# Attention scores as three bf16 matmuls of split operands instead of one f32 matmul

## The reference

```python
xn = layernorm(x)
def attn(x, norm_w, wq, k_of, v_of, wo, base, mask):      # H=16 heads of 64, 4 kv heads
    h = rmsnorm(x, norm_w)
    q, k, v = heads(h @ wq), heads(k_of(h)), heads(v_of(h))
    q, k = qk_norm(rope(q, base)), qk_norm(rope(k, base))
    scores = einsum('bhqd,bhkd->bhqk', q, repeat(k, 4)) / 8.0
    p = softmax(where(mask, scores, -1e30))
    return x + merge(einsum('bhqk,bhkd->bhqd', p, repeat(v, 4))) @ wo
s = attn(xn, ..., base=1e6, mask=causal)                  # global, k and v from a 256-wide latent
s = attn(s, ..., base=1e4, mask=causal & (i - j < 256))   # local, window of 256
ffn = _bitlinear(silu(_bitlinear(xn, w_gate)) * _bitlinear(xn, w_up), w_down)   # _aq(x) @ _wq(w).T
out = x + s * silu(ffn)
```

## Time and profile before

| | us |
|---|---|
| timed runs (2) | 7324.01 and 7516.66, median 7420.34 |
| profiled execution | 7373.87 |
| its slowest core, first to last instruction | 7372.3 |
| spans of the 8 cores | 7305.0 to 7372.3 |
| TensorE matmul busy | 4583.4 (62% of the span) |
| VectorE busy | 1800.2 (24%) |
| ScalarE busy | 1388.6 (19%) |
| mean granted TensorE clock of the cores | 0.730 to 0.738 |

### The profile page before, as it was taken

How to read it: one execution, slowest core, us unless ns; L and a number is a source line. 1 busy time by engine, 2 the same in 40 slices (tenths; PEclk the granted TensorE clock), 3 DMA queues, 4 the chain that set the end, 5 groups by cost and what they waited for, 6 DMA issues and landing times.

```text
span 7372.3 us, 43512 instructions; the slowest of 8 cores (7305.0 to 7372.3 us)
## 1 busy us (share of the span) xinstructions
PE 4583.4 (62%) x12414; PEld 1823.4 (25%) x12414; DVE 1800.2 (24%) x3044; ACT 1388.6 (19%) x2130; POOL 491.4 (7%) x420
## 2 busy tenths in 40 slices
PE   3567777878988898667777768680004263261734
PEld 0122222322332232222334333240001121120311
DVE  2222212111111111112313132223323441433422
ACT  1111202202312332011213021123321020100201
POOL 0000000000000000000000000000002312113120
PEclk6776777778888888777786868775556686685866
DMA  2100010010010000000010100007753133150423
GB/s 81 40 17 29 15 37 2 13 37 0 3 32 16 1 3 33 22 21 31 15 37 3 49 3 32 18 23 268 253 180 101 42 95 88 40 123 21 120 51 80
DMA packets 284199, 382.68 MB, mean 52 GB/s; under 512 B 144706, under 2 KB 225092, under 8 KB 276292
## 3 DMA queue, kind: packets, MB, share of 16 engines
q1 hardware_dynamic: 243652, 228.89, 10.7%
q0 software_dynamic: 40320, 151.02, 6.4%
HBM read 321.14 MB, written 50.33 MB: 50 GB/s over the span
## 4 chain that ended last, share of the span: by engine, by line
PE 57%; DMA 13%; DVE 12%; ACT 6%; issue 4%; POOLq 3%; DVEq 3%; POOL 1%; SPq 0%; ACTq 0%
PE pb L985 10%; PE pb L1020 7%; PE pb L854 7%; PE pb L892 7%; PE pb L1603 4%; POOLq L172 3%; PE pb L1031 3%; DMA fw<-wdq_scr 3%; PE pb L1070 3%; DVEq L172 2%; PE pb L648 2%; PE pb L587 2%; DMA fw<-wuq_scr 2%; PE pb L651 2%; PE pb L1469 2%
## 5 line engine op out<-in xcount | busy, mean ns | idle before, releaser
L985 PE MATMUL pb<-QT,KG 64*128 64x512 f32 (+3 forms) x1984 | 821.6, 556 | 69.3 <-DVEq L177 57.0
L854 PE MATMUL pb<-xst,wst 128*128 128x512 f32 x1024 | 508.0, 665 | 48.7 <-DVEq L177 41.2
L892 PE MATMUL pb<-AO,wst 128*128 128x512 f32 x1024 | 486.4, 641 | 54.1 <-DMA AO<-xst 54.1
L985 PEld LDWEIGHTS pb<-QT,KG 64*128 64x128 f32 x1984 | 373.9, 214 | 514.0 <-issue 476.3
L1603 PE MATMUL pb<-z,fw 128*128 128x512 f16 x1024 | 298.7, 463 | 264.5 <-DMA fw<-wdq_scr 219.9
L994 ACT ACTIVATE Pt<-pb,consts 128x512 f32<-128x512 f32 (+3 forms) x496 | 287.4, 587 | 664.6 <-PE pb L985 660.1
L1469 PE MATMUL pb<-z,fw 128*128 128x512 f16 x1024 | 313.5, 388 | 145.8 <-DVEq L177 88.4
L994 ACT ACTIVATE lat<-pb,consts 128x384 f32<-128x384 f32 (+3 forms) x496 | 266.9, 556 | 501.7 <-PE pb L985 495.1
L1006 DVE TENSOR_TENSOR Pt<-Pt,tb_mask_diag 128x128 f32<-128x128 f32 x256 | 74.8, 292 | 1021.4 <-ACT Pt L994 1018.7
L1475 PE MATMUL pb<-z,fw 128*128 128x512 f16 x1024 | 312.2, 387 | 0.0
L1070 PE MATMUL pb<-rows,tb_onesq 1*64 1x512 f32 x192 | 172.9, 1061 | 217.9 <-ACT rows L1059 193.2
(11 more groups left out here) (181 smaller groups left out, 4798.5 us busy)
## 6 DMA issues: line engine op xcount, KB each, us to landing
wf<-w_gate SPq DMA_DIRECT2D x16, 2048.0 KB, 9.4
wf<-w_up SPq DMA_DIRECT2D x16, 2048.0 KB, 10.0
wf<-w_down SPq DMA_DIRECT2D x64, 512.0 KB, 4.0
fw<-wdq_scr SPq DMA_DIRECT2D x32, 1024.0 KB, 6.6
wst<-g_wq POOLq DMA_DIRECT2D x32, 512.0 KB, 3.6
wst<-g_wo SPq DMA_DIRECT2D x32, 512.0 KB, 3.3
wst<-l_wq POOLq DMA_DIRECT2D x32, 512.0 KB, 3.6
wst<-l_wo SPq DMA_DIRECT2D x32, 512.0 KB, 3.2
```

The lines of the kernel that those rows point to most:

```text
L854: e.matmul(pb[oc], buf[:, oc * 128:(oc + 1) * 128], xst[:, kc * TW:(kc + 1) * TW], start=f, stop=g),
L892: e.matmul(pb[oc], buf[:, oc * 128:(oc + 1) * 128], AO[:, kc * TW:(kc + 1) * TW], start=f, stop=g),
L985: b=scb: e.matmul(b[0:128, qoff:qoff + N], lhsK, rhsQ, start=True, stop=True), inc="T")
```

## The change

The tiles KG and QT (f32) are replaced by KGh, KGl, QTh and QTl (bf16), of the same size in bytes together. A chunk of K or q is now copied from PSUM into AO (f32), normalized and rotated there, and then split: hi is its copy in bf16, lo is the chunk minus hi, in bf16. The function returns a further value, `split_v`, the commit behind the split; the first scores of kv 0 and of kv 1 wait for it. The score matmul becomes three bf16 matmuls that accumulate in the same bank: Kh·Qh, Kl·Qh, Kh·Ql. In the text the loads of the first two blocks of wo stand ahead of the eight q copies instead of behind them. Changes to debugging paths are left out here.

```diff
@@ -333,9 +334,11 @@
-    st["KG"] = kb.sbuf("KG", [128, 2 * st["s"]], F32, scoped=True)
+    st["KGh"] = kb.sbuf("KGh", [128, 2 * st["s"]], BF16, scoped=True)
+    st["KGl"] = kb.sbuf("KGl", [128, 2 * st["s"]], BF16, scoped=True)
...
-    st["QT"] = kb.sbuf("QT", [128, NC * TW], F32, scoped=True)
+    st["QTh"] = kb.sbuf("QTh", [128, NC * TW], BF16, scoped=True)
+    st["QTl"] = kb.sbuf("QTl", [128, NC * TW], BF16, scoped=True)
@@ -680,6 +685,15 @@  (end of rope_qknorm_sb)
     vfin = kb.commit("vector", "V")
+    if split_out is not None:
+        hi, lo = split_out
+        kb.op("vector", lambda e, ch=chunk, hi=hi: e.tensor_copy(hi, ch))
+        kb.drain("vector")
+        kb.op("vector", lambda e, ch=chunk, hi=hi, lo=lo: e.tensor_tensor(
+            lo, ch, hi, ALU.subtract))
+        spv = kb.commit("vector", "V")
+        return {"t_ind2": tt, "v_final": vfin, "split_v": spv,
+                "chunk_v": (deps["chunk_v"] if deps is not None else vfin)}
@@ -779,9 +794,11 @@  (the same at line 820, local)
             for oc in range(2):
-                kdeps = rope_qknorm(st, pb[4 + oc], t0,
-                                    KG[:, oc * s + t0: oc * s + t0 + TW],
-                                    deps=kdeps)
+                kdeps = rope_qknorm(
+                    st, pb[4 + oc], t0, AO[:, oc * TW:(oc + 1) * TW],
+                    deps=kdeps,
+                    split_out=(KGh[:, oc * s + t0: oc * s + t0 + TW],
+                               KGl[:, oc * s + t0: oc * s + t0 + TW]))
@@ -856,25 +875,29 @@
         kb.wait("vector", "T", kb.val("T"))
-        for oc in range(NC):
-            kb.op("vector", lambda e, oc=oc: e.tensor_copy(
-                QT[:, oc * TW:(oc + 1) * TW], pb[oc]))
-        qv = kb.commit("vector", "V")
         kb.guard("sync", "T")
         wo_toks = {0: kb.dma("sync", wst[:, 0:1024], wo[0:128, :], None),
                    1: kb.dma("sync", wst[:, 1024:2048], wo[128:256, :], None)}
+        for oc in range(NC):
+            kb.op("vector", lambda e, oc=oc: e.tensor_copy(
+                AO[:, oc * TW:(oc + 1) * TW], pb[oc]))
+        qv = kb.commit("vector", "V")
...
-            deps = rope_qknorm_sb(st, t0, QT[:, oc * TW:(oc + 1) * TW],
-                                  deps=deps)
-        emit_sdpa_kv(st, glob, t, 0, deep=False, qready=deps["v_final"])
+            deps = rope_qknorm_sb(
+                st, t0, AO[:, oc * TW:(oc + 1) * TW], deps=deps,
+                split_out=(QTh[:, oc * TW:(oc + 1) * TW],
+                           QTl[:, oc * TW:(oc + 1) * TW]))
+        emit_sdpa_kv(st, glob, t, 0, deep=False, qready=deps["split_v"])
...
-        emit_sdpa_kv(st, glob, t, 1, qready=deps["v_final"])
+        emit_sdpa_kv(st, glob, t, 1, qready=deps["split_v"])
@@ -981,9 +1007,15 @@
-            kb.op("tensor", lambda e, lhsK=lhsK, rhsQ=rhsQ, qoff=qoff, N=N,
-                  b=scb: e.matmul(b[0:128, qoff:qoff + N], lhsK, rhsQ,
-                                  start=True, stop=True), inc="T")
+            kb.op("tensor", lambda e, lhsKh=lhsKh, rQh=rQh, qoff=qoff, N=N,
+                  b=scb: e.matmul(b[0:128, qoff:qoff + N], lhsKh, rQh,
+                                  start=True, stop=False))
+            kb.op("tensor", lambda e, lhsKl=lhsKl, rQh=rQh, qoff=qoff, N=N,
+                  b=scb: e.matmul(b[0:128, qoff:qoff + N], lhsKl, rQh,
+                                  start=False, stop=False))
+            kb.op("tensor", lambda e, lhsKh=lhsKh, rQl=rQl, qoff=qoff, N=N,
+                  b=scb: e.matmul(b[0:128, qoff:qoff + N], lhsKh, rQl,
+                                  start=False, stop=True), inc="T")
```

More of the change, by code:

```diff
@@ L8 @@
 F16 = mybir.dt.float16
+BF16 = mybir.dt.bfloat16
 AF = mybir.ActivationFunctionType
@@ L380, in emit_all @@
             pairs = [(st["outT"][ch * 128:(ch + 1) * 128, 0:TW],
-                      st["QT"][:, ch * TW:(ch + 1) * TW]) for ch in range(NC)]
+                      st["QTh"][:, ch * TW:(ch + 1) * TW]) for ch in range(NC)]
         else:
@@ L398, in emit_all @@
         else:
-            pairs = [(st["outT"][0:128, :], st["KG"][:, 0:st["s"]]),
-                     (st["outT"][128:256, :], st["KG"][:, st["s"]:2 * st["s"]])]
+            pairs = [(st["outT"][0:128, :], st["KGh"][:, 0:st["s"]]),
+                     (st["outT"][128:256, :], st["KGh"][:, st["s"]:2 * st["s"]])]
         kb.dma_group("gpsimd", pairs, None)
@@ L618, in norm_tile, with rope_qknorm @@
     return kb.commit("vector", "V")
-def rope_qknorm(st, src_psum, t0, out_region, ncols=TW, deps=None):
+def rope_qknorm(st, src_psum, t0, out_region, ncols=TW, deps=None,
+                split_out=None):
     kb = st["kb"]
@@ L626, in rope_qknorm, with rope_qknorm_sb @@
         deps = dict(deps, chunk_v=vv)
-    return rope_qknorm_sb(st, t0, out_region, ncols, deps=deps)
-def rope_qknorm_sb(st, t0, chunk, ncols=TW, deps=None):
+    return rope_qknorm_sb(st, t0, out_region, ncols, deps=deps,
+                          split_out=split_out)
+def rope_qknorm_sb(st, t0, chunk, ncols=TW, deps=None, split_out=None):
     kb = st["kb"]
@@ L695, in emit_attn @@
     w, tb, c, pb = st["w"], st["tb"], st["consts"], st["pb"]
-    xn, KG, VG, QT, AO, lat, wst, xst = (st["xn"], st["KG"], st["VG"], st["QT"],
-                                         st["AO"], st["lat"], st["wst"], st["xst"])
+    xn, VG, AO, lat, wst, xst = (st["xn"], st["VG"], st["AO"], st["lat"],
+                                 st["wst"], st["xst"])
+    KGh, KGl, QTh, QTl = st["KGh"], st["KGl"], st["QTh"], st["QTl"]
     wq = w["g_wq" if glob else "l_wq"]
@@ L912, in emit_sdpa_kv @@
     kb, s = st["kb"], st["s"]
-    pb, pbh, tb, Pt, VG, KG, QT, AO = (st["pb"], st["pbh"], st["tb"], st["Pt"],
-                                       st["VG"], st["KG"], st["QT"], st["AO"])
+    pb, pbh, tb, Pt, VG, AO = (st["pb"], st["pbh"], st["tb"], st["Pt"],
+                               st["VG"], st["AO"])
+    KGh, KGl, QTh, QTl = st["KGh"], st["KGl"], st["QTh"], st["QTl"]
     Pt2 = st["lat"]
@@ L967, in emit_sdpa_kv @@
         last = (ci == L - 1)
-        lhsK = KG[rb:rb + 64, kcn * s + k0: kcn * s + k0 + 128]
         lhsV = ap_of(VG, (k0 // 128) * nblk + 65 * kv, [[vg_free, 128], [1, 65]])
+        lhsKh = KGh[rb:rb + 64, kcn * s + k0: kcn * s + k0 + 128]
+        lhsKl = KGl[rb:rb + 64, kcn * s + k0: kcn * s + k0 + 128]
         for j, (qc, half) in enumerate(pos):
@@ L972, in emit_sdpa_kv @@
             scb = pbh[sbanks[j]]
-            rhsQ = QT[qb:qb + 64, qc * TW + qoff: qc * TW + qoff + N]
+            rQh = QTh[qb:qb + 64, qc * TW + qoff: qc * TW + qoff + N]
+            rQl = QTl[qb:qb + 64, qc * TW + qoff: qc * TW + qoff + N]
             if ci == 0:
```

2 lines of the change are left out of this document (removed).

## The result

| | before | after |
|---|---|---|
| timed runs in this comparison | median 7582.52 us (10 runs, 7297.13 to 7703.76) | median 7258.68 us (11 runs, 7154.94 to 7532.63) |
| ratio after/before | | 0.9804, 95% interval 0.9773 to 0.9835 |
| the same two kernels measured again | | 0.9829, interval 0.9804 to 0.9855 |
| profiled execution | 7373.87 us | 7162.52 us |
| its slowest core's span | 7372.3 us | 7161.0 us |

The change makes the kernel 1.7 to 2.0% faster, just on the bound of 2%. Both medians stand far above the fastest runs (about 7290 and 7160 us), because in many executions one die runs at a lower granted clock, whatever the kernel; the ratio is made without these.

A forecast was written before the change was run, and what follows sets the result against it. TensorE's stream was taken to bound the kernel mid-kv, with score groups about 847 us. From 7373.9 us, minus 149 for shorter scores, plus 41 for exposed splits, came 7266 us, range 7180 to 7385.

The forecast's parts named there:

- The base: Whole kernel: the sum starts from the profiled execution, 7373.9 us; eight 512 groups of tile 1 noted at 0.81.
- Rival 3: Attention: bf16 scores hold the granted clock at 0.81, 200 us more than forecast, 7466 us; chance 0.07.
- The gain: Score groups in the attention: three bf16 matmuls replacing two f32 records save 149 us, bounds 99 to 198.
- 512, kv 0, 1.00: Score groups with only two score banks, 2.4 GHz: 3.99 us becomes 3.57, 0.42 saved, x24 = 10 us.
- 12 x 0.216: Score groups of 512 at 2.4 GHz: twelve bf16 matmuls of 0.216 us plus 0.19 make 2.78 us.
- two remainders of the f32 kernel: Score groups: 0.19 us step to the next kind of group, and 0.42 us from streamed score to exponential, both kept.
- The cost: VectorE after the ropes: 32 exposed splits of 1.27 us add 41 us, 49 at 1.54 each.
- the 48 splits: q chunks 0 to 2 and 4 to 6: hidden behind TensorE's next-chunk matmuls; without that cover 61 us.
- What moved in the text (the wo loads): Loads placed earlier in the text: SP waits only for T, its stream stays the same.
- Rival 1: Attention: larger gain, idle inside the groups goes too and more runs at 2.4 GHz; 174 less, 7200 us; chance 0.17.
- Rival 2: Attention: smaller gain, exponential and mask chains hold groups under 512, copy costs 0.69; 50 less, 7324 us; chance 0.13.
- Rival 4: Score matmuls: weight loads not hidden, costing 79 us (7345) or 220 us (7486); chance 0.08.

The follow-up runs named there:

- the undisturbed one: The kernel before, unchanged, profiled once more: 7292.2 us without any granted clock of 0.81, ratio to itself 0.9983.
- One bf16 product: The changed kernel with only Kh·Qh, one bf16 matmul per score, splits kept: ratio 0.9555 against the kernel before, profiled span 6965.4 us.
- two products: The changed kernel without Kl·Qh, two bf16 matmuls per score: ratio 0.9664 against the kernel before, profiled span 7025.5 us.
- One f16 product: The changed kernel with q and k written directly in f16, no split, one f16 matmul per score: four runs of 6941.9 to 7208.28 us, no ratio.
- the second profile of after: The changed kernel, unchanged, profiled and timed again beside the kernel before: ratio 0.9829, profiled spans 7135.4 to 7169.5 us.
- split alone: The kernel before with the split added to both ropes, written to unread scratch, first scores waiting for it, scores still f32: ratio 1.0051.

## Why the prediction was right or wrong

**The base: the step that failed.** The prediction made its sum against 7373.9 us and said of the 0.81 only that "Tile 1 shows a third level". That took the level for eight score groups and 8 us. Rival 3 asked whether the level could spread in the kernel after, but the prediction didn't ask what it had already cost in the base. (A misreading of no consequence: the page's PEclk goes from 6 to 8 tenths in slices 1 to 27, not from 5.) In truth 588 of that core's 7372 us ran at 0.81, and that execution was 80 us longer than the undisturbed one, mostly in the q and output projections, which the change doesn't touch. A sign stood in the trace: the q projection took 68.7 us in the four global tiles and 57 in the four local ones, for the same 128 records. Taking the sum against the kernel's own undisturbed level, 7292.2 - 149 + 41 = 7184, would have been 23 us above the 7161.0 measured; the 7266 of the forecast is 105 above it. That the median of the comparison, 7258.68, comes near 7266 is chance, for the reason given under the table of the result.

The Trainium skill (TensorE: Matmul & The Clock Gate, Seeing it yourself) gives 13/16 as a peak-current limit that takes a whole die once three of its cores run dense matmuls. The level agrees, 0.81. The rest of the rule doesn't agree with these traces: in the second execution of before all eight cores were as dense as ever and none was limited, and in the first, between 570 and 630 us of each core's own time, cores 6 and 2 of the same program stood thus:

```profile
570.00:630.00 60.00, 60.00 (x116) 25.50 (x115) 0.00 (x0) 0.00 (x0) 3.17 (x6) 0.81 0.17 53
...
570.00:630.00 60.00, 54.78 (x126) 23.75 (x124) 4.88 (x8) 0.63 (x1) 3.19 (x6) 0.98 0.20 70
```

The first is core 6, the second core 2, and cores 0 and 1, on core 2's die, stood at 0.87 and 0.88. Core 2 had none of the level before 4432 us of its own time, core 0 had it from 324 us on. In every profile that has the level, cores 0 and 1, 2 and 3, 4 and 5, 6 and 7 have their 0.81 stretches together and the pairs differ (668 and 685 us, 667 and 550, 435 and 400, 588 and 558 in before). What sets it off wasn't tried.

**The gain: right in mechanism, too small by 26 us.** Score groups from the start of their scores to the start of P·V, core 2, before without 0.81 against after:

| groups | before, us | after, us | forecast of one, after | sum, measured | sum, forecast |
|---|---|---|---|---|---|
| 512, own banks, 1.00 | 3.63 | 2.69 | 2.78 | -68 | -54, and -8 at 0.81 |
| 512, kv 0, 1.00 | 3.99 | 3.19 | 3.57 | -19 | -10 |
| 512, 0.50 | 7.11 | 5.45 | 5.4 | -24 | -27 |
| 384 | 2.77 (1.00) | 2.05 global, 2.23 local | 2.13 to 2.17 | -33 | -31 |
| 256 | 1.96 (1.00), 3.71 (0.50) | 1.76, 2.67 | 1.83, 2.8 | -22 | -15 |
| 128 | 1.64 (1.00) | 1.49 | 1.54 | -9 | -4 |
| all | 838.7 in sum | 663.6 in sum | | -175 | -149 |

The 12 x 0.216 of the earlier trace rows held exactly, and so did the doubling at 1.2 GHz, the 3.58 of P·V, and the chain that holds the narrow groups. Two terms were off.

The first is the tail behind a score, some 10 of the 26 us. The prediction carried two remainders of the f32 kernel over to bf16: 0.19 us for the step from scores to P·V, and 0.42 us from the end of a score's stream to its exponential. With bf16 they are 2.69 - 12 x 0.216 = 0.10 and 0.97 - 0.65 = 0.32. One bf16 product gives the same 0.32 (2244.08 - 2243.54 = 0.54, less 0.22), two products the same 0.10 (1.82 - 8 x 0.216), so it goes with the type and not with the number of passes. One f16 product gives the same as one bf16 product (0.54 us from score to exponential). The shorter step explains the 2.69 (72 groups x 0.09 = 6 us). The 256 and 128 groups with their own banks at 1.00 gave about 4 us beyond the forecast (0.20 per 256 group, forecast 0.13; 0.15 per 128 group, forecast 0.10); that this is the same tail, through the chain of score, exponential and mask, is likely and not shown by itself.

The second is kv 0, some 15 us: 9 in its 512 groups and 6 in its 256 and 128 groups (0.45 per 256 group at 1.00, forecast 0.13). In the 512 groups its second exponential was forecast to start 0.17 us after the first ended, as in before. That 0.17 was no cost of ScalarE, but a wait for the second f32 score, at 0.86 us a score. With scores every 0.65 us the exponentials run back to back, one row for two of them, and TensorE waits only once (kv 0 of tile 1, the first score, its exponential, the third and fourth score, P·V):

```profile
1080.63 0.39 PE L1011 MATMUL pb<-QTh,KGh 64*128 64x512 bf16 x1
...
1081.60 1.33 ACT L1026 ACTIVATE lat<-pb,consts 128x512 f32<-128x512 f32 x2 [5.09 <-PE pb L1017]
...
1082.43 0.37 PE L1011 MATMUL pb<-QTh,KGh 64*128 64x512 bf16 x1 [0.34 <-ACT lat L1026]
...
1083.08 0.37 PE L1011 MATMUL pb<-QTh,KGh 64*128 64x512 bf16 x1
...
1083.81 1.50 PE L1052 MATMUL pb<-lat,VG 128*65 128x512 f32 x3
```

The third score starts 1.80 us in (forecast 1.87), the fourth at 2.45 (2.73), P·V at 3.18 (3.57). So 0.21 of the 0.39 us is the missing gap, and the rest is the earlier first exponential (0.07) and the shorter step to P·V (0.11). For the narrow groups of kv 0 the waits were not taken apart. What is left of the 26 us, in the 384 groups and at 1.2 GHz, nearly cancels: the 384 groups gave 2 more, the 256 and 128 groups with their own banks at 1.2 GHz 2 more, the 512 groups at 1.2 GHz 3 less.

**The cost: right.** A split takes 1.30 us (forecast 1.27), the copy inside it 0.426 (taken from line 1342's 0.416) and not 0.69. The waits before the first score of kv 0 rose from 2.67 to 3.97 us, as forecast, and the stages with splits grew by about 37 us (41). That the 48 splits under the next chunk's swap matmul are free shows in the same sum: all 80 in the open would be 104 us. The Trainium skill (VectorE: DVE Perf Modes, Mode 2×_2P) has a single-source f32 operation from SBUF to SBUF run in a doubled mode where the PSUM one doesn't; the two rows, 0.43 for the cast and 0.69 for the copy from PSUM, agree.

**The sum again.** -175 in the score groups, about +37 for the splits: -138; measured -131 between the two undisturbed profiles, -123 with the second profile of after (7169.5). The 7 to 15 us left lie behind the attention, where the forecast had 0: from the last output projection to the end, the eight cores took 2387.6 us in the median in the undisturbed before, and 2400.5 and 2411.4 in the two profiles of after. The code there is the same in all runs, and the medians of the other profiles go from 2380 us (split alone) to 2412 (one product), so this is probably the executions' own spread and not the change's; what sets it wasn't tried. The stages from the end of a q projection to the output projection show where it went: 255.4, 372.6, 487.9 and 604.7 us in the global tiles 0 to 3 became 246.7, 350.8, 450.9 and 554.2, the gain growing with the number of 512 groups; the four local tiles gained 6.5, 11.2, 11.4 and 1.5 us (core 2). What moved in the text (the wo loads) left the engines' instruction lists as they were, as forecast: 0.

**The rivals.** Rival 1 (larger gain) was partly true: the stalls of kv 0 and of the narrow groups shrank, but the whole gain, 131, is nearer to the 108 of the forecast than to its 174. Rival 2 fell: no P·V of a 512 group waits for ScalarE until scores have one product only. Rival 3 (0.81 spreads with bf16) fell: 96 of the 96 groups behind the first of each kv ran at 1.00 in after, and the level appears in executions of both kernels. Rival 4 (loads in the open) fell: bf16 loads take 0.09 us and are hidden at a step of 0.216, all on the same 64 rows. One load between two matmuls of kv 0, tile 1:

```profile
1082.65 0.37 PE L1014 MATMUL pb<-QTh,KGl 64*128 64x512 bf16 x1
1082.65 0.09 PEld L1017 LDWEIGHTS pb<-QTl,KGh 64*128 64x128 bf16 x1
1082.86 0.37 PE L1017 MATMUL pb<-QTl,KGh 64*128 64x512 bf16 x1
```

The load for the matmul at 1082.86 runs from 1082.65, while the one before it streams. The rule of the Trainium skill (TensorE: Matmul & The Clock Gate, The mechanism) that only loads for other row groups overlap doesn't hold in these rows; the same section also names a background weight buffer that a load can go to ahead of time, and that reading agrees with them.

**The chances.** 0.67 for "within 2%" and 0.29 for "faster" were fair for a change of -1.7 to -2.0%; the bound runs through the middle of what was measured. The range in microseconds was not fair: with a base that was 80 us too long, the profiled execution of after and the fastest runs (7155 to 7177 us) lie below its lower end of 7180.
